# A product on GpSimd issued per group of 512 columns instead of per pair, and TensorE's wait split to match

## The chip, the cores and the metric

The kernel runs on one core of one Trainium2 chip. The metric is the device time of one execution in microseconds. Lower is better. Engines are named as in the profile: PE (TensorE), DVE (VectorE), ACT (ScalarE), POOL (GpSimd), SP (SyncE, which issues the DMAs).

## What is computed

Two parts, all in f32. The first is a stack of four Mamba layers over 64 context rows and 512 rows of x, for 16 sequences; the second is a block of cross attention with an MLP. The change lies in the first. Of its reference, cut to what matters here (DI = 512 channels, DS = 16 states):

```python
dA = jnp.exp(dt[..., None] * A)
dBu = dt[..., None] * Bm[:, :, None, :] * xi[..., None]

def step(h, t):
    da, dbu, c = t
    h = da * h + dbu
    return (h, jnp.einsum('bes,bs->be', h, c))
h0 = jnp.zeros((B, DI_, DS_), x.dtype)
_, ys = jax.lax.scan(step, h0, (dA.transpose(1, 0, 2, 3), dBu.transpose(1, 0, 2, 3), Cm.transpose(1, 0, 2)))
y = ys.transpose(1, 0, 2) + xi * Dp
y = y * jax.nn.silu(z)
return jnp.einsum('bse,de->bsd', y, op_w)
```

So every state runs through a linear recurrence along the sequence, is multiplied by its row of C, and the 16 products of a channel are summed.

## The kernel before, in words

A **group** is a tile of 128 channels by 512 time points for one of the 16 states. 512 channels are KI = 4 blocks c, so one layer of one sequence slot has G = 64 groups, handled as UNITS = 32 **pairs** v of groups 2v and 2v+1. One layer of one slot is a **step**. The kernel first walks 8 steps of a prefix phase (`pre`, the context rows, each slot holding 8 segments of 64), then 4 rounds of a main phase (16 steps each: 4 layers by 4 sequences), each round ending with the attention part for its 4 sequences.

Within a step, for each group g and pair v:

- ACT computes dA = exp(rate * dt) into a ring of 8 tiles (`decay_of`, L673).
- PE makes the input of pair v by products with a diagonal matrix that holds B (`make_input`, L437) in one of two PSUM buffers. It waits for the scans of the pair two before.
- DVE runs the scan of each group (`scan`, L912) into `hs`, a ring of 12 tiles (6 pairs), and counts `state_ready` up by one for each group.
- POOL multiplies hs by C in place (`product`, L1130 to L1140; the instruction is L1139): one instruction for the 1024 columns of a pair. It waits until both scans of the pair are done, and counts `product_ready` up by one for each pair.
- PE adds the products up (`sum_pair`, L442 to L458): eight transposing matmuls of 128 columns (L454) into one accumulator bank, four for each group, behind one wait for the pair's product (L451). At the first pair of a channel block it first adds the skip term by four transposes (L449).
- After 8 pairs ACT evicts the sum (L684).

Beside this stream every step carries the **events** of the steps before and after it, set by the tables at the top of the file, which say at which pair each engine does which: on PE the projections of the next step (xi L479, z L484, xp L490, dt L500), transposes (bT L494, dxT L505, yt L510) and the output projection (out L517); on ACT evictions, the softplus (L769 to L779), the skip scaling (L788), silu; on DVE the taps of the convolution (L940), softplus parts (L946 to L957), gate (L962). POOL has, at pairs 7, 15, 23 and 28 of a main step, the product dt * x of a channel block (`event`, L1159; called dtx3, dtx0, dtx1, dtx2), for which ACT's L788 and PE's L505 wait; and at pairs 24 to 31 one eighth of the next step's diagonal matrix each (`diag`, L1147). In the prefix it also keeps the last state of each segment (`keep`, L1127), ahead of each product, and the product waits for `keep`, since it overwrites hs. In the prefix dtx0 and dtx1 stand at pairs 27 and 30, dtx2 and dtx3 at pairs 1 and 4.

Every engine issues in the order in which this is written: within unit v of the loop PE does `make_input(v + 1)`, then the jobs of the table, then `sum_pair(v - 2)`; POOL does (`keep(v)`), `product(v)`, its event, then `diag`. SP reloads the C rows (`Crep`) for the next step in four DMAs, each behind the products that last read those rows (L1246).

Semaphore counts go through `Count`, whose second argument is how many increments a step makes.

## Time and profile before

| | us |
|---|---|
| median of 3 runs | 9753.22 (9751.4 to 9761.05) |
| profiled execution: its own time | 9749.7 |
| its span, first to last instruction | 9747.6 |
| busy, PE | 8898.7 (91%) |
| busy, DVE | 7469.1 (77%) |
| busy, POOL | 6517.7 (67%) |
| busy, ACT | 5984.7 (61%) |

The granted clock of TensorE is 0.962 of full speed on the mean of the span. The costliest groups are DVE's scan (5606.8 us, 1259 ns of one), POOL's product with C (5441.6 us, 2304 of them, 2366 ns of one) and the two matmul lines L437 and L454. "Busy" of an engine is the union of its instructions' recorded times, and an idle time is put down to the instruction whose semaphore event came last before it ended; that one need not be the one whose count was waited for.

### The profile page before, as it was taken

What the parts mean: (1) busy time and instruction counts of PE and PEld (TensorE: products, weight loads), DVE (VectorE), ACT (ScalarE), POOL (GpSimd) and SP (SyncE); (2) the same over time, 40 slices, a digit from 0 to 9 for tenths busy, and PEclk for the clock granted to TensorE, in tenths of its full rate; (3) what the DMA queues carried; (4) which work ended last, traced back from release to release, by engine and by line L of the source; (5) the groups of instructions that cost most, each with busy time, mean ns of one, the idle gap of its engine ahead of it and who ended that gap; (6) DMA issues with size and microseconds to landing.
All of it is one profiled execution on the core that took longest, in us unless ns stands there. A gap on an engine that the chain in (4) does not pass through costs nothing.

```text
span 9747.6 us, 188863 instructions
## 1 busy us (share of the span) xinstructions
PE 8898.7 (91%) x67488; PEld 6199.9 (64%) x67488; DVE 7469.1 (77%) x7810; ACT 5984.7 (61%) x9252; POOL 6517.7 (67%) x3556
## 2 busy tenths in 40 slices
PE   8999799999998799999988799999988799999988
PEld 5666466666664566666654576666654576666654
DVE  5778688888873588888873688888873688888872
ACT  6666576666743566676642566667642666766642
POOL 5878577788761477787751477887751577877750
PEclk9999899999999899999999899999999899999999
DMA  1111111111100111111100111111100111111100
GB/s 56 46 46 41 54 42 39 42 43 55 39 33 6 56 42 39 42 49 48 39 32 7 55 42 39 46 52 42 39 32 8 54 42 39 54 46 40 39 32 9
DMA packets 132793, 390.13 MB, mean 40 GB/s; under 512 B 49520, under 2 KB 77620, under 8 KB 94984
## 3 DMA queue, kind: packets, MB, share of 16 engines
q1 hardware_dynamic: 131848, 377.75, 11.0%
q8 instruction: 566, 9.27, 0.4%
q14 instruction: 379, 3.10, 0.1%
HBM read 364.46 MB, written 13.24 MB: 39 GB/s over the span
## 4 chain that ended last, share of the span: by engine, by line
POOL 48%; issue 38%; PE 3%; POOLq 1%; DVE 1%; ACT 0%; DVEq 0%; ACTq 0%
POOL arena L1139 40%; POOL arena L1147 5%; POOL arena L1159 2%; PE ps L540 1%; POOL arena L1177 1%; PE ps L621 1%; POOLq L1135 1%; DVE arena L1080 0%; DVE arena L1071 0%; ACT arena L824 0%; PE ps L587 0%; PE ps L616 0%; PE ps L517 0%; POOLq L314 0%; DVE arena L1084 0%
## 5 line engine op out<-in xcount | busy, mean ns | idle before, releaser
L1139 POOL TENSOR_TENSOR arena<-arena 128x1024 f32<-128x1024 f32 x2304 | 5441.6, 2366 | 1471.4 <-DVE arena L912 1428.0
L912 DVE TENSOR_TENSOR_SCAN arena<-arena,ps 128x512 f32<-128x512 f32 x4608 | 5606.8, 1259 | 763.1 <-PE ps L437 589.7
L673 ACT ACTIVATE arena<-arena,rate 128x512 f32<-128x512 f32 (+1 forms) x4608 | 3103.8, 713 | 782.7 <-DVE arena L912 771.0
L437 PE MATMUL ps<-arena 64*128 64x128 f32 x36864 | 2711.3, 287 | 345.7 <-DVE arena L912 343.0
L437 PEld LDWEIGHTS ps<-arena 64*128 64x128 f32 x36864 | 2266.8, 189 | 775.4 <-DVE arena L912 481.1
L454 PEld LDWEIGHTS ps<-csts,arena 128*128 128x128 f32 x18432 | 2133.2, 143 | 839.5 <-issue 622.5
L454 PE MATMUL ps<-csts,arena 128*128 128x128 f32 x18432 | 2462.4, 277 | 32.9 <-POOL arena L1139 32.9
L1159 POOL TENSOR_TENSOR arena<-arena 128x512 f32<-128x512 f32 x288 | 365.5, 1269 | 778.5 <-DVE arena L957 778.5
L1147 POOL TENSOR_TENSOR arena<-csts,arena 128x512 f32<-128x512 f32 x576 | 608.5, 1059 | 76.3 <-ACT arena L764 76.3
L788 ACT ACTIVATE arena<-arena,Dall 128x512 f32<-128x512 f32 x288 | 208.3, 723 | 719.3 <-POOL arena L1159 719.3
L517 PE MATMUL ps<-arena 128*128 128x512 f32 x1152 | 630.5, 641 | 7.6 <-DVE arena L962 4.4
L484 PE MATMUL ps<-arena 128*128 128x512 f32 x1152 | 634.7, 642 | 2.7 <-DVE arena L940 2.7
L479 PE MATMUL ps<-arena 128*128 128x512 f32 x1152 | 577.6, 628 | 34.0 <-DVE arena L922 33.4
L540 PE MATMUL ps<-arena 128*128 128x512 f32 (+2 forms) x1152 | 564.4, 646 | 31.7 <-ACT arena L884 16.2
L1177 POOL TENSOR_TENSOR arena<-arena 128x512 f32<-128x512 f32 x128 | 133.2, 1042 | 601.4 <-DVE arena L1074 601.4
L684 ACT ACTIVATE arena<-ps 128x512 f32<-128x512 f32 x288 | 170.8, 593 | 592.5 <-PE ps L454 591.8
L940 DVE SCALAR_TENSOR_TENSOR ps<-arena,ps 128x512 f32<-128x512 f32 x576 | 427.3, 742 | 90.4 <-ACT ps L727 86.8
L540 PEld LDWEIGHTS ps<-arena 128*128 128x128 f32 (+1 forms) x1152 | 240.7, 218 | 372.2 <-issue 350.0
L1106 DVE COPY arena<-ps 128x256 f32<-128x256 f32 x64 | 27.2, 425 | 478.2 <-PE ps L621 478.2
L824 ACT ACTIVATE arena<-ps 128x512 f32<-128x512 f32 (+1 forms) x252 | 137.5, 585 | 387.9 <-PE ps L540 319.5
L951 DVE SCALAR_TENSOR_TENSOR ps<-arena,ps 128x512 f32<-128x512 f32 x288 | 198.0, 687 | 193.5 <-ACT ps L779 192.8
L479 PEld LDWEIGHTS ps<-arena 128*128 128x128 f32 x1152 | 202.9, 195 | 224.7 <-issue 178.3
(102 smaller groups left out, 7640.7 us busy)
## 6 DMA issues: line engine op xcount, KB each, us to landing
arena<-c_rows SPq DMA_DIRECT2D x288, 1024.0 KB, 4.7
arena<-ip_x SPq DMA_DIRECT2D x20, 512.0 KB, 3.6
arena<-ip_z SPq DMA_DIRECT2D x20, 512.0 KB, 3.6
arena<-op_w SPq DMA_DIRECT2D x20, 512.0 KB, 3.9
hT<-xT SPq DMA_DIRECT2D x16, 512.0 KB, 5.2
arena<-w SPq DMA_DIRECT2D x8, 1024.0 KB
out<-arena SPq DMA_DIRECT2D x64, 128.0 KB, 1.7
arena<-xp_w SPq DMA_DIRECT2D x20, 160.0 KB, 2.5
```

The source lines that it names most:

```text
L437: i = nc.tensor.matmul(o, dtxT[rows, c, b, :], diagB[rows, pair, b, :].rearrange("p (i s) -> p i s", s=2), start=True, stop=True)
L454: i = nc.tensor.matmul(acc[:, b * P:(b + 1) * P], hs[:, place(n, v) + s, b * P:(b + 1) * P], eye, start=False, stop=(v + 1) % CU == 0 and ...
L479: i = nc.tensor.matmul(o, ipx[:, k, c * P:(c + 1) * P], xn[:, k, :], start=k == 0, stop=k == KD - 1)
L484: i = nc.tensor.matmul(o, ipz[:, k, c * P:(c + 1) * P], xn[:, k, :], start=k == 0, stop=k == KD - 1)
L517: i = nc.tensor.matmul(o, opw[:, k, c * P:(c + 1) * P], zs[:, par, k, :], start=k == 0, stop=k == KI - 1)
L540: last = nc.tensor.matmul(o, lhs, rhs, start=i == 0, stop=i == len(parts) - 1)
L673: nc.scalar.activation(o, i, ACT.Exp, scale=rate[:, ph.layer(n), g:g + 1]).then_inc(decay.sem, 1)
L912: nc.vector.tensor_tensor_scan(hs[:, place(n, v) + g % 2, :], dA[:, g % RING, :], both[:, g % 2::2], init[:, n % 2, g:g + 1] if ph.main() ...
L940: i = nc.vector.scalar_tensor_tensor(o, w, taps[:, c, k:k + 1], acc_c, ALU.mult, ALU.add)
L1139: nc.gpsimd.tensor_tensor(hs[:, a:a + 2, :], hs[:, a:a + 2, :], Crep[:, 2 * pair:2 * pair + 2, :], ALU.mult).then_inc(prod.sem, 1)
L1147: nc.gpsimd.tensor_tensor(diagB[:, pair, :, :].rearrange("p b (i s) -> p b i s", s=2), minus64.unsqueeze(1).unsqueeze(3).broadcast_to([P, ...
L1159: nc.gpsimd.tensor_tensor(dtx, dt[:, c, :], xs[:, m % 2, c, :], ALU.mult).then_inc(dtx_ready.sem, 1)
```

## The change

POOL's product is issued as two instructions for each pair, one for each group of 512 columns. Each waits for its own group's scan, and counts `product_ready` up by one, so that this semaphore now counts groups. TensorE waits for group 2v ahead of the first four transposes of `sum_pair` and for group 2v+1 ahead of the last four. SP's four waits of a step are rewritten to the same products in the new count. In the prefix both halves wait for `keep` of the pair, which still waits for both scans.

```diff
-        prod = Count(sem("product_ready"), UNITS)
+        prod = Count(sem("product_ready"), G)
...
-                pe.wait_ge(prod.sem, prod.at(ph, n, v + 1))
                 for s in range(2):
+                    pe.wait_ge(prod.sem, prod.at(ph, n, 2 * v + s + 1))
                     for b in range(NB):
                         i = nc.tensor.matmul(acc[:, b * P:(b + 1) * P],
                                              hs[:, place(n, v) + s, b * P:(b + 1) * P], eye,
...
             def product(ph, n, v):
 
-                pair = v % CU
                 if v < CU and v % 2 == 0:
                     pool.wait_ge(c_loaded[v // 2], ph.count(1, n, 1) * 16)
-                pool.wait_ge(state.sem, state.at(ph, n, 2 * v + 2))
-                if not ph.main():
-                    pool.wait_ge(kept_state.sem, kept_state.at(ph, n, v + 1))
-                a = place(n, v)
-                nc.gpsimd.tensor_tensor(hs[:, a:a + 2, :], hs[:, a:a + 2, :], Crep[:, 2 * pair:2 * pair + 2, :], ALU.mult
-                                        ).then_inc(prod.sem, 1)
+                for s in range(2):
+                    g, a = 2 * v + s, place(n, v) + s
+                    pool.wait_ge(state.sem, state.at(ph, n, g + 1))
+                    if not ph.main():
+                        pool.wait_ge(kept_state.sem, kept_state.at(ph, n, v + 1))
+                    nc.gpsimd.tensor_tensor(hs[:, a, :], hs[:, a, :], Crep[:, g % DS, :], ALU.mult).then_inc(prod.sem, 1)
...
-                        sp.wait_ge(prod.sem, prod.at(ph, n, UNITS - CU + 2 * k + 2))
+                        sp.wait_ge(prod.sem, prod.at(ph, n, G - DS + 4 * k + 4))
```

The order of POOL's instructions in a main step, from dtx1 (after pair 23) on, before:

```order
L1159 TENSOR_TENSOR arena<-arena 128x512 [waits job_done2,job_read2]
L1135 REGISTER_ALU
L1139 TENSOR_TENSOR arena<-arena 128x1024 [waits state_ready]
L314 REGISTER_ALU
L1146 REGISTER_ALU [waits job_read0]
L1147 TENSOR_TENSOR arena<-csts,arena 128x512 [waits input_ready]
L1135 REGISTER_ALU
L1139 TENSOR_TENSOR arena<-arena 128x1024 [waits state_ready]
```

and with the change, where the line numbers behind the product are one lower:

```order
L1158 TENSOR_TENSOR arena<-arena 128x512 [waits job_done2,job_read2]
L1136 REGISTER_ALU
L1139 TENSOR_TENSOR arena<-arena 128x512 [waits state_ready]
L1136 REGISTER_ALU
L1139 TENSOR_TENSOR arena<-arena 128x512 [waits state_ready]
L314 REGISTER_ALU
L1145 REGISTER_ALU [waits job_read0]
L1146 TENSOR_TENSOR arena<-csts,arena 128x512 [waits input_ready]
```

One 1024-column product with its register instruction has become two of 512 columns, each with one. The events and diags between the products stand where they stood.

On PE, one `sum_pair` of a main step between two `make_input`, before:

```order
L437 MATMUL ps<-arena 128x64x2 x7
L451 REGISTER_ALU
L454 MATMUL ps<-csts,arena 128x128 [waits product_ready]
L454 MATMUL ps<-csts,arena 128x128 x7
L432 REGISTER_ALU
```

and with the change:

```order
L437 MATMUL ps<-arena 128x64x2 x7
L452 REGISTER_ALU
L454 MATMUL ps<-csts,arena 128x128 [waits product_ready]
L454 MATMUL ps<-csts,arena 128x128 x3
L454 MATMUL ps<-csts,arena 128x128 [waits product_ready]
L454 MATMUL ps<-csts,arena 128x128 x3
L432 REGISTER_ALU
```

The fifth of the eight transposes now carries a wait, and no instruction is added.

## Rows read from the trace of the kernel before

**Rows 1.** Windows (busy us by engine, clock, DMA): prefix, last prefix, main step

```profile
435.11:554.32 119.21, 111.74 (x918) 81.98 (x916) 95.13 (x99) 80.10 (x122) 96.27 (x79) 0.96 0.13 46
904.50:1005.30 100.80, 89.08 (x861) 72.17 (x857) 82.67 (x78) 47.32 (x73) 93.40 (x75) 0.96 0.10 28
2427.63:2538.48 110.85, 106.59 (x889) 77.59 (x888) 96.88 (x97) 77.09 (x119) 88.01 (x45) 0.98 0.12 45
```

**Rows 2.** Timeline of DVE, main step: start, length, instruction [idle before <-releaser]

```profile
2508.93 7.13 DVE L912 TENSOR_TENSOR_SCAN arena<-arena,ps 128x512 f32<-128x512 f32 x6
...
2537.03 1.55 DVE L940 SCALAR_TENSOR_TENSOR ps<-arena,ps 128x512 f32<-128x512 f32 x2 [0.29 <-ACT ps L727]
2538.48 1.27 DVE L912 TENSOR_TENSOR_SCAN arena<-arena,ps 128x512 f32<-128x512 f32 x1
```

**Rows 3.** Timeline of ACT in the same step

```profile
2515.06 0.72 ACT L788 ACTIVATE arena<-arena,Dall 128x512 f32<-128x512 f32 x1 [2.93 <-POOL arena L1159]
...
2529.30 1.33 ACT L673 ACTIVATE arena<-arena,rate 128x512 f32<-128x512 f32 x2
2531.94 0.72 ACT L788 ACTIVATE arena<-arena,Dall 128x512 f32<-128x512 f32 x1 [1.31 <-POOL arena L1159]
...
2536.24 0.75 ACT L727 ACTIVATE ps<-ps,arena 128x512 f32<-128x512 f32 x1
```

**Rows 4.** Timeline of POOL in the same step, pairs 23 to 28

```profile
2511.45 2.36 POOL L1139 TENSOR_TENSOR arena<-arena 128x1024 f32<-128x1024 f32 x1 [0.58 <-DVE arena L912]
2513.76 1.27 POOL L1159 TENSOR_TENSOR arena<-arena 128x512 f32<-128x512 f32 x1
2514.99 2.37 POOL L1139 TENSOR_TENSOR arena<-arena 128x1024 f32<-128x1024 f32 x1
2517.31 1.05 POOL L1147 TENSOR_TENSOR arena<-csts,arena 128x512 f32<-128x512 f32 x1
...
2524.97 2.38 POOL L1139 TENSOR_TENSOR arena<-arena 128x1024 f32<-128x1024 f32 x1
...
2528.29 2.39 POOL L1139 TENSOR_TENSOR arena<-arena 128x1024 f32<-128x1024 f32 x1
2530.61 1.29 POOL L1159 TENSOR_TENSOR arena<-arena 128x512 f32<-128x512 f32 x1
2531.84 1.07 POOL L1147 TENSOR_TENSOR arena<-csts,arena 128x512 f32<-128x512 f32 x1
```

**Rows 5.** Timeline of PE in the same step, two places

```profile
2494.92 0.60 PE L449 MATMUL ps<-csts,arena 128*128 128x128 f32 x4
2495.36 1.04 PE L454 MATMUL ps<-csts,arena 128*128 128x128 f32 x8
2496.32 1.16 PE L437 MATMUL ps<-arena 64*128 64x128 f32 x16
...
2529.33 1.09 PE L454 MATMUL ps<-csts,arena 128*128 128x128 f32 x8
```

**Rows 6.** Timeline at the end of a round's last step

```profile
2838.61 5.97 DVE L912 TENSOR_TENSOR_SCAN arena<-arena,ps 128x512 f32<-128x512 f32 x5
2839.97 7.03 POOL L1139 TENSOR_TENSOR arena<-arena 128x1024 f32<-128x1024 f32 x3 [0.58 <-DVE arena L912]
...
2847.05 1.09 PE L454 MATMUL ps<-csts,arena 128*128 128x128 f32 x8 [1.24 <-POOL arena L1139]
```

**Rows 7.** Timeline of POOL, then PE, in a prefix step

```profile
532.10 1.06 POOL L1147 TENSOR_TENSOR arena<-csts,arena 128x512 f32<-128x512 f32 x1
533.09 0.23 POOL L1127 COPY arena<-arena 128x16 f32<-128x16 f32 x1
533.46 2.37 POOL L1139 TENSOR_TENSOR arena<-arena 128x1024 f32<-128x1024 f32 x1
535.79 1.05 POOL L1147 TENSOR_TENSOR arena<-csts,arena 128x512 f32<-128x512 f32 x1
...
544.54 1.10 PE L505 MATMUL ps<-csts,arena 128*128 128x128 f32 x4 [2.66 <-POOL arena L1159]
```

## The prediction

> **What bounds the kernel now.** I first read the busy table and the windows: a step of the main part takes 110.85 us and PE works in 106.59 of them, DVE in 96.88, POOL in 88.01; a step of the first part (prefix) takes 119.21 us, with POOL at 96.27; in the last prefix step POOL works in 93.40 of 100.80 us [rows 1]. No engine is full in the main step, so the question is which waits lie on the way from one step's first scan to the next one's. The chain view is no help: it follows POOL back through every product and puts the gaps down to "issue". I therefore followed the timeline, asking at each instruction which of its waits, by the counts in the code, was met last.
>
> Going back from the first scan of a main step: it stands behind two taps on DVE that waited 0.29 us for ScalarE's L727 [rows 2]. ScalarE had worked without a pause since 2531.94, when the skip scaling (L788) was let go by POOL's event product (L1159) after 1.31 us of idling [rows 3]. That product (pair 28's event, dtx2) stood in POOL's queue: from 2511.45 to 2530.61 POOL does six products, one dtx and four diags without a pause [rows 4]. This run begins where POOL waited 0.58 us for a scan, the second of pair 23. Further back the chain is scans and matmuls, with no POOL in it. All main steps that prepare a next step look alike: 15 in each of the 4 rounds, 60.
>
> TensorE's sums look as if they waited for POOL in the table of waits, but the counts say otherwise: sum_pair(v) is issued two units after scan v and behind the next inputs, and in the main steps its first transpose starts at least 2 us after the product's end. The product of pair 27 runs 2524.97 to 2527.35 [rows 4], its sum starts at 2529.33 [rows 5]. So the finer wait on TensorE brings nothing there. What can bring something is that POOL's half may start one scan earlier; what can cost is that POOL has an instruction more for each pair.
>
> **The price of a half.** No row shows a 512-column product with C. The nearest is the event product L1159: the same multiplication of two full f32 tiles, 512 columns. What matters in a queue that never pauses is the spacing of starts: 1.23 us after L1159 (2513.76 to 2514.99, 2530.61 to 2531.84), 2.32 after the 1024-column product (2514.99 to 2517.31) [rows 4]. I take 1.225 for a half, h below, so a pair costs 2h - 2.32 = 0.13 us more. Bounds: 1.16 (half of 2.32, no price of an instruction at all) and 1.27 (the recorded length of L1159). By recorded lengths (1.27 and 2.37) a pair would cost 0.17 more. The Trainium skill (Trace Analysis, GPSIMD Engine Instruction) says to time POOL instructions by the spacing of starts, since recorded spans there are unreliable. The trace agrees in that 2513.76 + 1.27 lies behind the next start. By the lengths the sum below would be about -4 us, by the spacings -20; I go by the spacings.
>
> **Term A, the POOL run of the main step.** Before, product 23 starts at 2511.45 when its second scan is done; dtx1 follows at 2513.76. After: the first half can start once the first scan of the pair is done (scans 23a and 23b are the first two of six from 2508.93 [rows 2]; 23a is done near 2510.2 and POOL idles then), the second at 2511.45, and dtx1 at 2511.45 + h, which is 2.31 - h = 1.085 us earlier. Then five pairs (24 to 28) cost 0.13 each, 0.65. dtx2 starts 0.43 us earlier. Would a scan now bind in between? The tightest is pair 27, started at 2524.97 and now about 0.7 earlier, at 2524.3; its first half needs only the first scan, and its second, due at 2525.5, has its scan by 2524.97. No. Can the end use 0.43? ScalarE idled 1.31 us before L788 [rows 3], and DVE 0.29 before the taps [rows 2]; but the DVE work ahead of the taps descends, through L779 and L784, from the skip that waits for dtx1 (2515.06 [rows 3]), and that one comes 1.085 earlier. A chain to the next step that touches POOL nowhere is about 1.1 us shorter than the bound one, by my adding up of the margins along it, for which no single row stands; 0.43 fits. **60 x 0.43 = -26 us.**
>
> **Term B, the end of each round.** In the last step of a round PE does wait for products: products 29 to 31 run from 2839.97 for 7.03 us, and the last sum starts at 2847.05 after 1.24 us of idle [rows 6]. The scans from 2838.61 (five in 5.97, 1.19 each) let the halves start: 29b at 2839.97, then h by h, 31b ends at 2839.97 + 5h = 2846.10 instead of 2847.00, 0.9 us earlier; and four of the last eight transposes (0.11 each [rows 5]) are done before it, 0.44. **4 x 1.35 = -5 us.**
>
> **Term C, the prefix.** There every product stands behind keep (L1127), which waits for both scans of the pair, and is let go by keep's own end: 0.37 us from keep to product, 0.99 from diag to keep, 2.33 from product to diag [rows 7]. So no half starts earlier, and the 0.13 is paid wherever POOL is the bound. It is: PE's L505 waits 2.66 us for dtx [rows 7]. Following the waits, nine products lie on the chain of each of the 7 steps between prefix steps (five before this dtx0, four before the next dtx1), and about 31 in the last one, where POOL is nearly full: 94 pairs x 0.13 = **+12 us**.
>
> **Term D, the rest.** SP's counts are rewritten to the same moments. PE gets 2304 more waits, all met long before in the main steps. What a met wait costs between transposes is shown at L449 to L454: four transposes from 2494.92, then eight, the first of which waits for a product: 0.44 us for four, the same 0.11 each as without a wait [rows 5]. The eight take 0.96 us to L437's start, 0.09 more than 8 x 0.109; I put that to the change of the tile's height, from 128 rows to 64, since L437 to a job that waits for nothing shows it too. **0.** The register instructions that POOL gains run on its sequencer while the engine works. Products that end about 1.1 us earlier where POOL had been waiting for scans only lengthen POOL's and ScalarE's idle time.
>
> **Sum:** with all terms in h, 60(13.9 - 11h) - 5 + 94(2h - 2.32), about 848h - 1059 (the 94 pairs and 60 steps drive it): -20 us at h = 1.225, and 8.5 us for every 0.01 us of h. The profiled execution took 9749.7 (span 9747.6), the median of the three is 9753.22; so **9733 us**, 0.2% less. A measurement of this kernel can tell 0.2% (about 20 us) from no change, so my forecast sits on that edge.
>
> **The rivals.**
> 1. *A half is really half* (h 1.16 to 1.19). Then product 23 gives 1.15 and little is lost after it; the gain per step is capped at 1.1 us by the POOL-free chain: 60 x 1.1 + 5 = 71 us less, or 50 less at h = 1.19: 9682 to 9703. For it: L1159 writes another tile and is only a relative. Against: a copy of 16 columns takes 0.37 us to the next start, its wait included [rows 7], so an instruction is not free. The Trainium skill (GPSIMD Engine Reference, Instruction dispatch) gives the dispatch of an instruction as tens of cycles; taking 40 at 1.2 GHz, an estimate, h would be 1.18 and the time within this rival's. Chance 0.17.
> 2. *The gain stops at the next wait*: some DVE work ahead of the taps does not come earlier, and only the 0.29 us of its idle time, or h near 1.24, is gained: 60 x 0.15 to 0.27 gained, 5 more by B, 12 lost by C: 2 to 9 us less, 9744 to 9751. Chance 0.26.
> 3. *POOL becomes slower than before*: a half costs 1.27 or more, because of the second semaphore update, register step and start. It decides from h = 1.25. At 1.27 it is 848 x 1.27 - 1059 = +18, 9771; at 1.29, +35, 9788. For it: the recorded length. Against: the spacing. Chance 0.16.
> 4. *PE pays for the wait.* Some 20 sums of a main step lie on the chain; 0.09 us for each would be 1.8 x 60 = +108 on top of the -20, 9841. Against: L449 to L454. Chance 0.03.
>
> The forecast has 0.38, and spans 9722 to 9743 (h from 1.213 to 1.237). Half of it lies beyond the 0.2% edge. Faster by over 0.2%: 0.17 of rival 1, 0.19 of the forecast and 0.05 for a larger share of B and A than counted here, 0.41. Slower by over 0.2% (from h = 1.27 on): 0.09 of rival 3 and 0.03 of rival 4, 0.12. Within: 0.47. The range leaves out 2 in 10: the lower half of rival 1 (0.08) and those 0.12, so 9690 to 9768.
>
> **What would show it.** The product group at L1139 (the line stays) should have 4608 members of 1.27 us, spaced 1.22 in the run of a main step; the main step 110.4 us instead of 110.85; prefix steps about 1.1 us longer; L788's wait before dtx2 0.9 instead of 1.31; L454 spaced 0.11 throughout its eight. It is wrong if the half's spacing is off by over 0.03, if the main step keeps 110.85 although dtx2 starts earlier, or if PE shows a gap between the fourth and fifth transpose.

## The result, and the profile after

The changed kernel takes **9714.76 us** (median of 6 runs, 9710.72 to 9722.3) against 9752.31 us before (6 runs, 9746.38 to 9761.05): a ratio of 0.9962 with a 95% interval of 0.9949 to 0.9975. It is 37.5 us faster; 20 were forecast (9733 us), the range was 9690 to 9768. The forecast's own branch was 9722 to 9743 and rival 1's 9682 to 9703, so the measured time lies between the two, in neither. The profiled execution's span went from 9747.6 to 9712.9, 34.7 less.

The page of the changed kernel, engines and groups (busy us, mean ns of one, idle before and its releaser):

```profile
PE 8902.0 (92%) x67488; PEld 6194.1 (64%) x67488; DVE 7467.3 (77%) x7810; ACT 5988.0 (62%) x9252; POOL 6846.0 (70%) x5860
...
L1139 POOL TENSOR_TENSOR arena<-arena 128x512 f32<-128x512 f32 x4608 | 5765.3, 1276 | 1143.4 <-DVE arena L912 1103.9
```

POOL works 328 us more than before and the kernel is faster, so busy time alone would have pointed the other way. The reading that matters is the length of a step, from first scan to first scan. Windows of three consecutive main steps of the changed kernel (length, busy us of PE, PEld, DVE, ACT, POOL with counts, granted clock, DMA):

```profile
2101.67:2211.70 110.03, 105.22 (x890) 76.49 (x889) 96.81 (x97) 77.15 (x120) 92.60 (x77) 1.00 0.11 40
2211.70:2321.74 110.04, 105.17 (x890) 76.44 (x889) 96.85 (x98) 77.11 (x120) 92.59 (x77) 1.00 0.15 51
2321.74:2432.78 111.04, 107.97 (x891) 78.43 (x889) 96.93 (x98) 77.27 (x120) 92.66 (x77) 0.97 0.11 41
```

and of three before:

```profile
2316.78:2427.64 110.86, 105.21 (x889) 76.47 (x888) 96.89 (x98) 77.09 (x119) 87.92 (x45) 1.00 0.11 40
2427.64:2538.48 110.84, 106.58 (x889) 77.59 (x888) 96.87 (x97) 77.09 (x119) 88.00 (x45) 0.98 0.12 45
6789.80:6901.38 111.58, 108.11 (x889) 78.47 (x888) 97.00 (x97) 77.08 (x119) 87.98 (x45) 0.97 0.12 44
```

In what follows an **inner step** is one of the 13 steps of each round that are neither its first nor its last two, 52 in all, and it is **undisturbed** when TensorE's granted clock is full throughout.

Two things stand in these rows. An undisturbed inner step went from 110.85 to 110.03, twice what was forecast (0.43). And in every third step (16 of 52) the granted clock is at its lower level for 6.8 us, and the step is 0.8 to 1.0 us longer. Before, the clock fell in every second step (25 of 52). In 22 of these it stayed low for only 3.4 us, and they are as long as the others; in three it stayed low for 6.8 us, and they are 0.7 to 1.0 longer, as the third row shows.

Cut at the first scans, the difference of the two traces comes out as follows:

| part | before | after | difference | forecast |
|---|---|---|---|---|
| start to the first main scan (prefix) | 1099.05 | 1109.88 | +10.8 | +12 |
| 60 main steps that prepare a next one | | | -36.4 | -26 |
| 4 last steps of a round, attention included | 522.93, 522.69, 523.45, 443.87 | 520.48, 519.86, 521.67, 441.76 | -9.2 | -5 |
| sum | | | -34.7 | -20 |

POOL in the first of the three steps, pair 23 to dtx2 (start, length, instruction, count, idle before), answering to [rows 4]:

```profile
2183.85 2.51 POOL L1139 TENSOR_TENSOR arena<-arena 128x512 f32<-128x512 f32 x2 [0.50 <-DVE arena L912]
2186.31 1.27 POOL L1158 TENSOR_TENSOR arena<-arena 128x512 f32<-128x512 f32 x1
2187.53 2.50 POOL L1139 TENSOR_TENSOR arena<-arena 128x512 f32<-128x512 f32 x2
2189.99 1.05 POOL L1146 TENSOR_TENSOR arena<-csts,arena 128x512 f32<-128x512 f32 x1
...
2203.86 1.31 POOL L1158 TENSOR_TENSOR arena<-arena 128x512 f32<-128x512 f32 x1
```

Two halves take 2.46 from start to start, so h = 1.23 and a pair costs 0.14 more than the 2.32 of before. dtx1 to dtx2 takes 17.55 (2186.31 to 2203.86) against 16.85, which is five times 0.14. Both can be counted from the start of the first scan of pair 23, which is the first of these six:

```profile
2182.50 7.12 DVE L912 TENSOR_TENSOR_SCAN arena<-arena,ps 128x512 f32<-128x512 f32 x6
```

dtx1 stands 3.81 behind it, before it was 4.83 (2508.93 to 2513.76 [rows 2] [rows 4]): 1.02 earlier. dtx2 stands 21.36 behind it in place of 21.68: 0.32 earlier. ACT's L788 now waits longer for dtx2, not shorter:

```profile
2205.20 0.72 ACT L788 ACTIVATE arena<-arena,Dall 128x512 f32<-128x512 f32 x1 [1.93 <-POOL arena L1158]
```

It was 1.31 [rows 3]. The step gained 0.82 and dtx2 only 0.32, so dtx2 was not what bound the step before. Where the other chain enters is seen 12 us into the next step. DVE of the kernel before, next step begun at 2538.48:

```profile
2549.21 1.27 DVE L912 TENSOR_TENSOR_SCAN arena<-arena,ps 128x512 f32<-128x512 f32 x1
2550.84 0.76 DVE L940 SCALAR_TENSOR_TENSOR ps<-arena,ps 128x512 f32<-128x512 f32 x1 [0.35 <-ACT ps L727]
```

and of the changed kernel, next step begun at 2211.70:

```profile
2222.44 1.27 DVE L912 TENSOR_TENSOR_SCAN arena<-arena,ps 128x512 f32<-128x512 f32 x1
2223.63 0.73 DVE L940 SCALAR_TENSOR_TENSOR ps<-arena,ps 128x512 f32<-128x512 f32 x1
```

The tap at +12.36 used to wait 0.35 for ScalarE; at +11.93 it waits for nothing. DVE had time left between the first scan of a step and this tap, so the first scan, and with it all that led to it through dtx2, was not binding.

In the prefix, POOL from keep on, answering to [rows 7]:

```profile
532.19 0.22 POOL L1127 COPY arena<-arena 128x16 f32<-128x16 f32 x1
532.55 2.50 POOL L1139 TENSOR_TENSOR arena<-arena 128x512 f32<-128x512 f32 x2
535.02 1.05 POOL L1146 TENSOR_TENSOR arena<-csts,arena 128x512 f32<-128x512 f32 x1
```

Keep to product 0.36 as before, the pair 2.47 in place of 2.33.

At the end of a round's last step, TensorE (answering to [rows 6]; POOL does seven halves from 2840.76 on without a pause):

```profile
2846.99 0.66 PE L454 MATMUL ps<-csts,arena 128*128 128x128 f32 x4 [0.57 <-POOL arena L1139]
...
2849.44 0.66 PE L454 MATMUL ps<-csts,arena 128*128 128x128 f32 x4 [0.57 <-POOL arena L1139]
2850.95 0.63 PE L510 MATMUL ps<-csts,arena 128*128 128x128 f32 x4 [0.86 <-ACT arena L684]
```

Each half of a sum starts as its product ends. L510 stands 90.66 after the step's first scan in all four rounds, where it stood at 91.6 in three rounds before and at 90.9 in the fourth.

### The profile page after: what moved, and what is told of

It reads as the page before. It is cut to its first block, busy times and chain, and to the rows that moved or that the text cites. A ratio compares the mean times of both kernels' runs of the same rounds, so it can differ in the third digit from the quotient of the medians.

```text
span 9712.9 us, 193419 instructions
## 1 busy us (share of the span) xinstructions
PE 8902.0 (92%) x67488; PEld 6194.1 (64%) x67488; DVE 7467.3 (77%) x7810; ACT 5988.0 (62%) x9252; POOL 6846.0 (70%) x5860
## 4 chain that ended last, share of the span: by engine, by line
POOL 51%; issue 36%; PE 3%; POOLq 1%; DVE 1%; ACT 0%; DVEq 0%; ACTq 0%
POOL arena L1139 43%; POOL arena L1146 4%; POOL arena L1158 2%; PE ps L540 1%; POOL arena L1176 1%; POOLq L1136 1%; PE ps L621 1%; DVE arena L1080 0%; DVE arena L1071 0%; ACT arena L824 0%; PE ps L517 0%; PE ps L587 0%; PE ps L437 0%; PE ps L616 0%; PE ps L454 0%
## 5 line engine op out<-in xcount | busy, mean ns | idle before, releaser
L1139 POOL TENSOR_TENSOR arena<-arena 128x512 f32<-128x512 f32 x4608 | 5765.3, 1276 | 1143.4 <-DVE arena L912 1103.9
L437 PE MATMUL ps<-arena 64*128 64x128 f32 x36864 | 2710.8, 287 | 313.8 <-DVE arena L912 306.4
L437 PEld LDWEIGHTS ps<-arena 64*128 64x128 f32 x36864 | 2266.9, 189 | 745.9 <-DVE arena L912 445.9
L1158 POOL TENSOR_TENSOR arena<-arena 128x512 f32<-128x512 f32 x288 | 365.6, 1269 | 777.4 <-DVE arena L957 777.4
L517 PE MATMUL ps<-arena 128*128 128x512 f32 x1152 | 639.2, 649 | 7.6 <-DVE arena L962 4.4
L540 PE MATMUL ps<-arena 128*128 128x512 f32 (+2 forms) x1152 | 559.7, 642 | 31.7 <-ACT arena L884 16.2
L788 ACT ACTIVATE arena<-arena,Dall 128x512 f32<-128x512 f32 x288 | 208.0, 722 | 582.8 <-POOL arena L1158 582.6
L1176 POOL TENSOR_TENSOR arena<-arena 128x512 f32<-128x512 f32 x128 | 133.2, 1042 | 593.9 <-DVE arena L1074 593.9
L940 DVE SCALAR_TENSOR_TENSOR ps<-arena,ps 128x512 f32<-128x512 f32 x576 | 425.3, 738 | 100.3 <-ACT ps L727 96.6
L500 PE MATMUL ps<-arena 33*128 33x512 f32 x576 | 323.2, 642 | 2.8 <-DVE arena L957 2.8
```

What stands on the lines that cost most here:

```text
L437: i = nc.tensor.matmul(o, dtxT[rows, c, b, :], diagB[rows, pair, b, :].rearrange("p (i s) -> p i s", s=2), start=True, stop=True)
L517: i = nc.tensor.matmul(o, opw[:, k, c * P:(c + 1) * P], zs[:, par, k, :], start=k == 0, stop=k == KI - 1)
L540: last = nc.tensor.matmul(o, lhs, rhs, start=i == 0, stop=i == len(parts) - 1)
L940: i = nc.vector.scalar_tensor_tensor(o, w, taps[:, c, k:k + 1], acc_c, ALU.mult, ALU.add)
L1139: nc.gpsimd.tensor_tensor(hs[:, a, :], hs[:, a, :], Crep[:, g % DS, :], ALU.mult).then_inc(prod.sem, 1)
L1158: nc.gpsimd.tensor_tensor(dtx, dt[:, c, :], xs[:, m % 2, c, :], ALU.mult).then_inc(dtx_ready.sem, 1)
```

## The experiments

**The theory (T).** Two chains bound a main step before. C1 leaves POOL at dtx1, goes through L788, ScalarE, DVE and TensorE and reaches the next step at the tap of +12.4: 110.85. C2 goes through POOL's whole run to dtx2 and L788 to the step's first scan: 110.41. With the change dtx1 comes 1.08 earlier by the count (1.02 by the rows above; C1: about 109.8), dtx2 only 0.37 (0.32 by the rows; C2: 110.03), and C2 binds. **The rival (R)** is the prediction's view: the run binds alone, and the greater gain comes from elsewhere, the prefix's or TensorE's waits or the slack of single scans.

In the kernels that keep whole products (e1 to e3, e5, e6 and e8 to e10) such a product counts two at once, `then_inc(prod.sem, 2)`, so that TensorE and SyncE wait for the same counts as in the change. In their text a whole product is L1139, a half L1147, a diag L1154 and a dtx L1166 (e10: four higher behind its own edit). The diffs are cut, and against the changed kernel; e9's and e10's leave out what stood in an earlier one, and e8 is e6 with e7's two lines. Step lengths and falls of the clock are those of one profiled execution of each kernel, times are medians.

### e1: halves in the main part alone

```diff
+                if not (ph.main()):
...
+                    nc.gpsimd.tensor_tensor(hs[:, a:a + 2, :], hs[:, a:a + 2, :], Crep[:, 2 * pair:2 * pair + 2, :],
+                                            ALU.mult).then_inc(prod.sem, 2)
+                    return
```

> Halves in the main phase only; in the prefix the product stays one instruction for each pair, counting up by two. Both theories of the main phase leave its steps as with the change (110.03 us, every third 111.03). If the prefix pays 0.14 us for each pair on its chain, the first main scan, at 1109.88 us with the change and 1099.05 before, comes back to about 1099, and the time is 11 us below the change: 9704. If the prefix lost its 10.8 us to something else (the finer wait on TensorE), it stays near 1109.

9705.12 us (9703.42 to 9706.78), ratio 0.9954 [0.9937, 0.997]. The first main scan is back at 1100.18, undisturbed steps take 110.04. So the prefix costs what Term C said, and the gain is all of the main part. The main part of e1 is the change's, instruction for instruction, and yet the clock first falls at +89.6 and +90.5 us in the last steps of rounds 1 and 4, where with the change it fell at +132 and +103. This bears on e4 and e9.

### e2: halves at the pairs ahead of dtx0, dtx1 and dtx3 alone

```diff
+                if not (ph.main() and v in (7, 15, 23)):
```

> Halves only at pairs 7, 15 and 23 of a main step, those ahead of an event product; all other products whole. Theory T (two chains bound the step: one through dtx1 alone, 110.85 us before, and one through the whole POOL run 23 to 28, 0.44 shorter): dtx1 and dtx2 both come 1.08 earlier and no pair pays; the step is 109.8 us, or less if the first chain has other ends. Theory R (the POOL run alone bounds, as in the prediction): 110.85 - 1.08 = 109.8 as well. Both: 52 inner steps at 109.8 plus what the lower clock adds; the prefix as before; about 9752 - 60 x 1.05 + up to 20 = 9690 to 9710. A theory by which halves help because all pairs are finer would leave it near 9752.

9744.92 us (9739.03 to 9750.29), 0.9995 [0.9985, 1.0004]. Undisturbed steps 110.43, not 109.8. The clock falls in 24 of the 52 inner steps; in 19 of them it stays low for 6.8 us, and these are 0.7 to 1.2 longer. POOL shows why the head is not gained:

```profile
4578.60 2.37 POOL L1139 TENSOR_TENSOR arena<-arena 128x1024 f32<-128x1024 f32 x1 [0.59 <-DVE arena L912]
4580.93 2.50 POOL L1147 TENSOR_TENSOR arena<-arena 128x512 f32<-128x512 f32 x2
4583.39 1.27 POOL L1166 TENSOR_TENSOR arena<-arena 128x512 f32<-128x512 f32 x1
```

The first half of pair 23 has no wait before it in this trace: pair 22, still whole, keeps POOL busy until 4580.93, when the first scan of pair 23 had long been done. The second half starts 1.23 behind it, 0.8 after its own scan's end, and dtx1 gains 0.41 (4.42 behind the pair's first scan) in place of 1.08. The expectation had left out the pair in front. The step gains what dtx1 gains, 0.42. All three entries are in halves here, so that C1 starts at dtx1 and not at dtx0 or dtx3 is read from the trace and was not tested.

### e3: halves in the run 24 to 28 alone

```diff
+                if not (ph.main() and 24 <= v <= 28):
```

> Halves only at pairs 24 to 28 of a main step: the price of the halves on the POOL run without the gain at its head. Theory T: the chain through dtx1 is untouched at 110.85, the one through the run was 110.41 and gets 5 x 0.142 = 0.71 longer, 111.12; the step grows by 0.27 us, 60 steps 16 us: 9768. Theory R (the run itself was the bound): 0.71 for each step, 111.56, 43 us: 9795. If POOL's run is not on any bounding chain: 110.85 and 9752.

9785.16 us (9779.42 to 9788.92), 1.0035 [1.0021, 1.0049]. This is the run that separates the two views, by its step and not by its time. Window of one step, the scans that begin with pair 23's, and the two dtx on POOL:

```profile
2211.60:2322.72 111.12, 105.33 (x890) 76.49 (x889) 96.86 (x98) 77.05 (x120) 88.75 (x50) 1.00 0.15 52
```

```profile
2292.44 7.12 DVE L912 TENSOR_TENSOR_SCAN arena<-arena,ps 128x512 f32<-128x512 f32 x6
...
2297.33 1.26 POOL L1166 TENSOR_TENSOR arena<-arena 128x512 f32<-128x512 f32 x1
...
2314.91 1.27 POOL L1166 TENSOR_TENSOR arena<-arena 128x512 f32<-128x512 f32 x1
```

The run became 0.73 longer (17.58 against 16.85), the step only 0.27 (111.12 against 110.85). The missing 0.46 is the slack that C2 had. R expected 111.56, T 111.12: T stands. Counted from pair 23's first scan, dtx2 stands at 22.47 here, at 21.68 before and at 21.36 with the change. If C2 binds here, at 111.12, it took 110.33 before and takes 110.01 with the change, where the undisturbed step takes 110.03.

The time is 17 above T's 9768, for two reasons that T did not hold. In 14 of the 52 inner steps the clock stays low for 6.8 us and they take 0.8 to 1.1 more, and the last steps of the rounds take 8.6 more in sum than before. This step is longer than that of the kernel before, so it is not the shorter step that brings the costly falls.

### e4: TensorE waits for both halves of a pair

```diff
+                pe.wait_ge(prod.sem, prod.at(ph, n, 2 * v + 2))
                 for s in range(2):
-                    pe.wait_ge(prod.sem, prod.at(ph, n, 2 * v + s + 1))
```

> The change with POOL's halves everywhere, but TensorE waits for both halves ahead of the first transpose, as before. If the main steps gain by POOL's start alone, they stay at 110.03 and 111.03 us, and only places where TensorE really waits for POOL lose: 0.44 us at the end of each round and at the end of the prefix, some 2 to 3 us in all, 9717. If a part of the gain came from the finer wait on TensorE, the main steps move back towards 110.85, up to 9750.

9729.63 us (9725.71 to 9734.54), 0.9979 [0.9969, 0.9989]: 14.9 slower than the change, where 2 to 3 were expected. Inner steps are the same on the mean (110.33), but the four last steps take 525.68, 523.71, 523.76 and 444.03, 13.4 more in all. TensorE at a round's end:

```profile
2847.15 1.09 PE L454 MATMUL ps<-csts,arena 128*128 128x128 f32 x8 [1.08 <-POOL arena L1139]
2849.59 1.79 PE L454 MATMUL ps<-csts,arena 128*128 128x128 f32 x8 [1.35 <-POOL arena L1139]
...
2854.20 6.16 PE L517 MATMUL ps<-arena 128*128 128x512 f32 x7 [0.87 <-DVE arena L962]
```

Four transposes fewer lie before the last product's end, as Term B counted (0.44). L510 comes 0.86 later in three rounds and 1.56 in the first, whose last eight transposes take 1.79 in place of 1.09 at the lower clock. Most of the rest lies where the clock is low: it first falls 89.8 to 91.4 us into the step in all four rounds, where with the change it fell at 103 or 132, and the first eight matmuls of the output projection take 6.0 in place of 3.67. That the longer pauses (1.08 and 1.35 in place of 0.57) brought this on is not shown. The kernel before has pauses of 1.25 and 1.24 at this place, and in three of its rounds the clock first fell at +104.5; e1 has the change's pauses of 0.57, and in two of its rounds the clock fell at +89.6 and +90.5.

### e5 and e6: the full head, and the run whole

e5 has halves at the two pairs ahead of each dtx, e6 everywhere but in the run:

```diff
+                if not (ph.main() and (v in (6, 7, 14, 15, 22, 23) or n == ph.steps - 1 and v >= 28)):
```

```diff
+                if not (ph.main() and not 24 <= v <= 28):
```

> Main part only: halves at pairs 6, 7, 14, 15, 22, 23 (the two ahead of each dtx) and from pair 28 on in the last step of a round; whole products elsewhere and in the prefix. The theory of two chains (one through dtx1 alone, 110.85 before; one through POOL's whole run to dtx2, 110.41 before): product 22 is now in halves too, so 23a starts with its scan and dtx1 comes the full 1.08 earlier, and no half in the run costs anything: the two chains are 109.8 and 109.3, so undisturbed steps take 109.8, 0.6 less than with halves at 23 alone (110.42) and 0.2 less than with the change (110.03). Time about 9705 less the prefix's nothing, 9690 to 9700 if a third of the steps has its spell of low clock, up to 9720 if every second has. Rival (halves at the entry bring no more than e2's 110.42, because something else bounds): 110.4, about 9740.

> Main part: halves for all pairs but 24 to 28, which stay whole; prefix whole. The theory of two chains expects of undisturbed steps the same 109.8 as of the run before it, since further halves elsewhere lie under waits for scans; the last steps of a round as with the change (520.0 against 522.9 before). Time 9690 to 9700. Rival (product halves outside the entries cost 0.14 each on the path): 110.0 or more, 9705 or more.

e5 9706.89 us (9704.5 to 9709.28), 0.9951 [0.9935, 0.9968]; e6 9708.56 us (9704.53 to 9712.06), 0.9955 [0.9938, 0.9972]. Both show the same undisturbed step, 109.96 to 109.98: below the 110.03 of the change, not 109.8. Since they agree, the further halves of e6 cost the step nothing, though its time is the one that its rival named (9705 or more). POOL of e6:

```profile
3574.07 1.27 POOL L1166 TENSOR_TENSOR arena<-arena 128x512 f32<-128x512 f32 x1
...
3582.20 2.37 POOL L1139 TENSOR_TENSOR arena<-arena 128x1024 f32<-128x1024 f32 x1 [0.19 <-DVE arena L912]
...
3591.18 1.27 POOL L1166 TENSOR_TENSOR arena<-arena 128x512 f32<-128x512 f32 x1
```

Started 1.08 earlier, the run of whole products meets its scans: pair 26 waits 0.19 for its second one (in e5 it starts 1.11 behind the diag ahead of it, where others start 1.00 behind). dtx1 to dtx2 takes 17.11, 0.44 less than with the change, and the step is only 0.07 shorter. So something bounds it that is 0.1 to 0.2 longer than C1 and C2 now are, and T had not seen it. Followed back from pair 26, its scans wait for their input, L437, and from there it is TensorE's own queue without a pause for some 60 us: a third chain, C3, in which neither dtx1 nor the head of the run stands. This is argued from the trace; no run changes C3 alone. The tap at +12.3 waits 0.33 for ScalarE again, as in the kernel before, so what binds enters the next step there and not at its first scan. The same 109.97 is found in e8, e9 and e10. Steps with a fall of the clock are 17 and 16 of 52; the 15 and 16 in which it stays low for 6.8 us are 0.7 to 1.1 longer.

### e7: extra matmuls in TensorE's pauses

What a third of the steps shows is best seen side by side. TensorE of the changed kernel in an undisturbed step (the first is 16.5 us into the step):

```profile
2228.22 1.16 PE L437 MATMUL ps<-arena 64*128 64x128 f32 x16 [1.83 <-DVE arena L912]
2229.31 1.09 PE L454 MATMUL ps<-csts,arena 128*128 128x128 f32 x8
2231.75 1.16 PE L437 MATMUL ps<-arena 64*128 64x128 f32 x16 [1.35 <-DVE arena L912]
2232.84 1.13 PE L517 MATMUL ps<-arena 128*128 128x512 f32 x2
```

and at the same place one step later:

```profile
2338.24 1.16 PE L437 MATMUL ps<-arena 64*128 64x128 f32 x16 [1.83 <-DVE arena L912]
2339.34 1.65 PE L454 MATMUL ps<-csts,arena 128*128 128x128 f32 x8
2341.78 2.08 PE L437 MATMUL ps<-arena 64*128 64x128 f32 x16 [0.79 <-DVE arena L912]
2343.79 2.07 PE L517 MATMUL ps<-arena 128*128 128x512 f32 x2
```

The same work in the same order, nearly twice as long: the granted clock is at its lower level (1.2 of 2.4 GHz) from 2339.72 to 2346.54. It falls 1.5 us after the end of a pause of 1.83, and lasts into work that has no pause behind it. In the kernel before, in the step that begins at 2427.64, it is low from 2445.44 to 2448.86:

```profile
2445.90 1.97 PE L454 MATMUL ps<-csts,arena 128*128 128x128 f32 x8
2448.15 1.48 PE L437 MATMUL ps<-arena 64*128 64x128 f32 x16 [0.28 <-DVE arena L912]
2449.56 1.12 PE L517 MATMUL ps<-arena 128*128 128x512 f32 x2
```

There the slower transposes lie in the wait for the next scan (0.28 are left of 1.35), the clock is back before the work without pauses begins, and the step loses nothing. So it is in all eight traces so far (before, with the change, e1 to e6): the 30 inner steps with a low stretch of 3.4 us are as long as the undisturbed ones within 0.1, the 114 with one of 6.8 us are 0.7 to 1.2 longer. What the change made worse is how often the long stretch comes, 16 of 52 in place of 3. e7 fills the two pauses: matmuls that write again what they have just written, in the main part only.

```diff
-                for b in range(NB):
+                for b in (list(range(NB)) * 2 if ph.main() and v == 5 else range(NB)):
...
-                    for b in range(NB):
+                    for b in (list(range(NB)) * 3 if ph.main() and c == 3 else range(NB)):
```

> The change, and on TensorE in the main steps the 16 matmuls of the input of pair 5 issued twice and the four transposes of channel block 3's y three times (24 matmuls of 128x128 or 64x128 too many, about 3 us of work, the same results written again). They lie in the pauses of TensorE ahead of +18 us of a step. If the spells of low clock come from those pauses, no inner step shows a lower granted clock and all take 110.03 in place of 110.03, 110.03, 111.03: 16 us less than the change, about 9697. Rival (the spells have another cause, or the extra work lengthens the path): spells stay or steps grow by up to 3 us, 9713 or more.

9716.9 us (9715.49 to 9718.77), 0.9961 [0.9947, 0.9975]: no faster than the change, and yet the mechanism is shown. Its TensorE at the same place, and one window:

```profile
2230.12 2.06 PE L437 MATMUL ps<-arena 64*128 64x128 f32 x32 [0.95 <-DVE arena L912]
...
2233.66 1.16 PE L437 MATMUL ps<-arena 64*128 64x128 f32 x16 [0.46 <-DVE arena L912]
```

```profile
2323.68:2433.71 110.03, 106.97 (x914) 78.23 (x913) 96.80 (x97) 77.13 (x120) 92.72 (x77) 1.00 0.12 41
```

No inner step of the 52 has a lower clock, their mean is 110.05 against 110.33, and the 60 steps take 16.2 us less, as expected. Two other places took it back. The last steps of the rounds became 13.9 longer in sum (525.40, 521.48, 525.20, 445.54), since eight of the extra transposes stand on the path there and three rounds had the lower clock again from +89.5; and the prefix, whose code is that of the change, took 4.7 more in this execution. The line that was edited for its place at +15 us of a step runs at a round's end too, where it stands on the path.

### e8: e6 with the extra matmuls

> The main halves without 24 to 28, prefix whole, and the same extra matmuls. By both theories together all inner steps take 109.8: 60 times 0.25 less than the change with extra matmuls, and 11 less in the prefix: about 9675 to 9682. If the extra matmuls do nothing for the clock: as the kernel without them, 9690 to 9700.

9692.89 us (9689.12 to 9694.85), 0.9936 [0.992, 0.9953]. Inner steps 109.97, none at a lower clock; 15.7 less than e6. In the traces the 60 steps take 14.4 less, with the same undisturbed step, so this is the clock. It is above the 9675 to 9682 expected by the misses of e5 (0.16 a step) and e7 (the last steps of the first three rounds 522.7 to 522.9).

### e9: the extra transposes taken out of the last step, halves in all of it

```diff
+                if not (ph.main() and (n == ph.steps - 1 or not 24 <= v <= 28)):
...
+                    for b in (list(range(NB)) * 3 if ph.main() and c == 3 and m < ph.steps - 1 else range(NB)):
```

> Whole products in the prefix and at pairs 24 to 28 of the main steps, halves elsewhere and in all of a round's last step; the repeated matmuls as in the two runs before it, but not the eight transposes too many of the last step of a round, where they stood on the path. Theory of the clock: inner steps 109.97 as in the last run; the last step's first L510 at +90.7 in place of +91.05, with four transposes in place of twelve, and the low clock not before +103: 520 in place of 522.9, so 2.5 to 2.9 less in each of four rounds, about 9682. Rival (the low clock near +91 comes whatever the end of the step looks like, since it depends on what the engine did before): 522.5, about 9691 to 9693.

9692.92 us (9688.54 to 9693.53), 0.9935 [0.9919, 0.9952]: as e8, the rival was right. L510 starts at +90.73 as expected, but the clock falls at +90.5 in every round although the end of this step has the change's own instructions:

```profile
2830.47 0.66 PE L454 MATMUL ps<-csts,arena 128*128 128x128 f32 x4 [0.57 <-POOL arena L1147]
2831.98 1.09 PE L510 MATMUL ps<-csts,arena 128*128 128x128 f32 x4 [0.86 <-ACT arena L684]
2833.95 5.96 PE L517 MATMUL ps<-arena 128*128 128x512 f32 x8 [0.88 <-DVE arena L962]
```

With the change it fell at +103 or +132, and in e1, whose main part is the change's, at +90 in two rounds and at +132 in the other two. So the same pauses may come with the lower clock or not; what decides was not found.

### e10: e9, and TensorE's pauses at the round's end filled

```diff
+                    if ph.main() and n == ph.steps - 1 and (v, s) in ((30, 1), (31, 0), (31, 1)):
+                        for b in range(NB):
+                            nc.tensor.matmul(input_ps[:, 0, b * P:(b + 1) * P], eye, eye,
+                                             start=True, stop=True, is_transpose=True)
```

> The run before it and, in the last step of a round, four transposes of the identity into an input bank that is free, after the second half of the sum of pair 30 and after each half of the sum of pair 31 (12 in a round, 48 in all), which fill TensorE's pauses of 0.57 and 0.86. If those pauses bring on the low clock near +91, none of the four last steps shows it before +100, and the last steps take 520 as the best of the change; time 9682 or as the run before it if that has no low clock there. If it makes no difference: the same first low-clock times as the run before it.

**9678.01 us** (9676.98 to 9682.26), 0.992 [0.9903, 0.9936]: the fastest of all, 75 us under the kernel before (9753.36 in these runs) and 37 under the change. In the text of this kernel L460 are the idle transposes, and lines behind the edit are four higher (L514 is L510, L521 is L517):

```profile
2837.78 0.66 PE L454 MATMUL ps<-csts,arena 128*128 128x128 f32 x4
2838.27 0.60 PE L460 MATMUL ps<-csts 128*128 128x128 f32 x4
2839.29 0.63 PE L514 MATMUL ps<-csts,arena 128*128 128x128 f32 x4 [0.42 <-ACT arena L688]
2840.80 3.67 PE L521 MATMUL ps<-arena 128*128 128x512 f32 x8 [0.88 <-DVE arena L966]
```

L514 starts at +90.75 as in e9 and the attention's first matmul at +102.5 in place of +105.3; the clock first falls at +132 to +135. Last steps 519.10, 519.91, 519.71 and 439.63: 13.7 less than e9, by 12 idle transposes in a round.

### e11: the kernel before with e7's extra matmuls

> The kernel before with the repeated matmuls (16 of the input of pair 5, and yt3's four transposes three times). In it the spells of low clock cost nothing as the trace shows (110.84 to 110.94 with or without), so the theory expects inner steps of 110.85 as before, without spells, and at the rounds' ends 1 to 2 us more each for the eight transposes on the path: 9750 to 9758. Rival (the repeated matmuls shorten the step by themselves, not by the clock): inner steps under 110.6, 9735 or less, and the gain of the last runs over the change would not be the change's spells.

9747.9 us (9745.61 to 9752.19), 0.9992 [0.9983, 1.0002]. All inner steps 110.84 to 110.95, with no lower clock in any of them. The extra matmuls do nothing to the path of these steps by themselves; what they brought in e7 and e8 is the clock. It also confirms that before the change its fall had cost little inside the main steps (mean 110.91 against 110.87, by the three steps with a long low stretch).

## Why the prediction was right, and where it was off

- **The price of a half: right.** 1.231 from start to start against 1.225; by the formula's 8.5 us for every 0.01 that moves the sum by 5 us, to -15. (In the sum's line 60(13.9 - 11h) lacks its minus; the closed form, 848h - 1059, has it.) The recorded length (1276 ns) would have misled, as the text said. The 0.14 that a pair costs is the fixed part of a POOL instruction here. The Trainium skill (GPSIMD Engine Reference, Instruction dispatch) gives the one indirect call in the dispatch of an instruction as tens of cycles; at the 1.2 GHz that the prediction used, 0.14 us are some 170 (an estimate). So the 40 cycles of the prediction's estimate are well below what this product pays, and the measured price speaks against rival 1.
- **Term C, the prefix: right.** +10.8 against +12; the mean first main scan of ten executions with whole products there is about 1100, of the three with halves about 1112. Single executions scatter by some 4 us around it, so whether 94 is the right count of pairs cannot be told.
- **Term D, a wait that is met costs nothing: right** for the main steps. e4's inner steps agree with the change's to 0.01.
- **Term A, the main step: direction right, size wrong.** The step that failed is "Going back from the first scan of a main step": I followed one chain from scan to scan, took the POOL run to dtx2 as bound, and credited the step with dtx2's 0.43. Both dtx moved much as counted (dtx1 1.02 against 1.085, dtx2 0.32 against 0.43), but the undisturbed step became 0.82 shorter. The prediction had itself found that a chain not touching POOL was about 1.1 us shorter, but not that the chain through dtx1 alone was 0.44 longer than the one through the run. Its sign stood in the trace: the tap at 2550.84 waits 0.35 for ScalarE, 12.36 us into the next step, and no chain that starts from the first scan can see it. e3 shows the slack of the run directly: 0.73 on the run cost the step 0.27.
- **What the prediction did not have at all: the clock.** With the change TensorE's clock stays low for 6.8 us in every third step, at 1.0 each and about 16 us over the kernel (e7). Why it does so more often than before is not known; the shorter step is not the reason, since e3, whose step is longer, has it in 14 of 52. Without these falls Term A would have been some -50. The miss in the chain and the miss in the clock have opposite signs, and so the total came nearer to the forecast than its parts: that the time lies in the stated range is in part luck.
- **Term B, the round's end: -5 forecast, -9.2 measured.** The earlier products and the split sum move L510 forward by 0.95 in three rounds and 0.27 in the fourth, 3.2 in sum where 5 were counted. The other 6 us lie behind it, where the clock fell later than before (at +132, +132, +103 and +103, in place of +104.5 three times and +88), and the sum had no term for the clock. e4 gives the split wait 3.4 a round in place of 0.44, but most of that is where the clock falls, and e1 shows that this differs between rounds of the same instructions. So of the -9.2 the part beyond L510's 3.2 may be luck of this execution.
- **The rivals.** 2, the gain stops at the next wait, was nearest in kind: there is a next wait, but behind a greater gain. 1 had the nearer time (9703 at its slow end), but its reason, a half that costs half, is refuted by the 1.231. 3 and 4 did not happen. "The main step 110.4", and "L788's wait before dtx2 0.9", under what would show it, were both wrong (110.03 and 1.93), and the second of them is the sign by which a reader of the new trace finds the mistake.

Still open: what decides whether the clock falls at a round's end (e1 and e9 against the change, e4 against the kernel before), and why it stays low for 6.8 us in the changed kernel's steps and mostly for 3.4 in those before. That e7, e8, e10 and e11 remove it by filling pauses is shown; the rule behind it was not tried.

## What to carry to other kernels

A loop whose steps overlap has more than one chain from step to step, and they need not enter the next step at the same instruction: look for waits well behind its first instruction too, and price an edit on every chain that it touches. A queue's head gains from finer pieces (its successor starts one piece earlier), its full stretches pay the fixed price of each piece; so split only ahead of what others wait for, the pair in front of it included. When TensorE has pauses, compare the granted clock of each stage before and after, and how long each low stretch is: filling pauses with matmuls that change nothing was worth 15.7 us inside the steps (e6 to e8) and 14.9 at the rounds' ends (e9 to e10), together nearly as much as the change itself.

## What the runs showed of the hardware that I had not expected

- TensorE lost half its clock shortly after a pause of 1.83 us inside a step in which it works 105 of 110 us. In the changed kernel this came in one step of three, though all have this pause, and cost 1.0 us each time. A low stretch of 6.8 us cost 0.7 to 1.2 in every kernel traced, one of 3.4 us at the same place at most 0.1. The Trainium skill (TensorE: Matmul & The Clock Gate, What's actually happening) says that the throttled state is the default and activity releases it. The runs agree in that more activity, even useless, kept the clock: 24 extra matmuls in a step took it from falling in 16 of 52 steps to none.
- Extra matmuls in a pause cost nothing on the path: the kernel before with them has the same 110.85.
- POOL's 512-column product costs 1.231 from start to start, the 1024-column one 2.32: 1.09 for each 512 columns and 0.14 for the instruction.
